# Gated linear attention and a mixture of experts: side jobs of the attention steps stand elsewhere in each engine's order

## Chip, cores and metric

One core of a Trainium2 chip. The metric is the device time of one execution in microseconds (us). Three runs of the kernel before gave 1457.93, 1460.13 and 1462.41 us.

## The reference

```
h = layernorm(x) * (1 + ca) + sa                      # x: 32 x 256 x 128; shifts, scales, gates from c and wmod
q, k, v = h @ W_q, h @ W_k, h @ W_v                   # 16 heads of 64
a = sigmoid(h @ W_gate + b_gate)
S_t = a_t * S_(t-1) + k_t v_t^T ;  o_t = q_t S_t      # a scan over the 256 tokens, per head
x = x + ga * (o @ W_o)
h = layernorm(x) * (1 + cb) + sb
x = x + gb * (shared_expert(h) + sum over the best 2 of 8 experts of weight * expert(h))
```

The recurrence is not run token by token. For chunks of 128 tokens the running products of the gates (F) and their inverses (G) scale queries and keys, and the recurrence becomes masked attention: scores of scaled keys and queries, a causal mask, and a product with the values.

## The kernel before

**Steps and rounds.** The 32 batches have 8 pairs of heads each. One *step* handles two head pairs of one batch, so a batch has 4 steps (`DUOS`, e = 0 to 3), and a *round* of two batches has 8 (s = 0 to 7). 16 rounds make 128 steps, numbered d. Rounds 0, 1, 2 and 15 are written out, 3 to 14 are a loop on each engine. After them a tail finishes the routing and runs the experts block by block.

Every engine has its own order of work, written by hand in its own `round_of_steps`; they meet only through semaphores, and an engine runs in order. A step d is a pipeline over the engines:

- TensorE (PE): attention of step d-1 (`attend`, L1637, into `vo_bank`), scores of step d (L1622), gates of step d+2 (`project_z`, L1534 to L1536 into `z_bank`), queries and keys of step d+1 (`project_qk`, the same lines into `qk_banks`), values (L1577 to L1579, into `vo_bank`) and the output projection of step d-1 (L1648, into `y_bank`). Before the values it waits until ScalarE has copied the attention out of `vo_bank` (`s_o`).
- VectorE (DVE): `first_head` (masked copy of the first head's scores, L1196, L1198), `products` (scaled keys and queries, L1188; they wait for `project_qk`), `scans` (G in L1176, F in L1181, for step d+2).
- ScalarE (ACT): copy of the attention (L767), second head's scores (L785, L786), exponents (L746) and tanh (L752) of the gates, copy of the values (L758), scaled keys for the second chunk (L779).
- GpSimd (POOL): causal mask of the second head (`mask_second_head`, L510; `attend` waits for it), `growth` (L600), `gates` (L593 after the exponents, L595 after tanh; the scans wait for them).
- SyncE (SP) moves rows between memories, one round at a time.

**Side jobs** stand inside these steps. They are the normalisation of the next batch (e = 0 and 1: `normalise`, two transposes L1531, `h_attention` L763, `split_h`) with `moments` and `inverse_std`, and the routing of finished batches: `moments2`, `inverse_std2`, `normalise2` (L1108) and `h_rows` (L567 to L571) make the second layer norm, `h_transposed` (L1531, copied by ACT in L792) transposes it at s = 6 and 7, `router` (L1594, s = 0) and `logits` (L1115) give logits, `logits_exp` (L576) their exponentials, `choose` and `weigh` (s = 3) the two experts of a token and their weights, `ranks` (PE, L1600 to L1607, s = 4) and `places` (DVE, L1156 to L1168, with `next_row` in L1160) the row each token goes to. ACT writes the first expert into the rows (`write_first_expert`, L816, L817), and POOL scatters them with 8 indirect DMAs a round (`scatter_rows`, L584). `update_x` (L614, L617) adds the attention's output to x.

The products of five of these jobs (two normalisations, two transposes of rows, the router, and the ranks) go into `vo_bank`, which the values then take. So PE waits for the engine that reads them (`s_hf`, `s_hc`, `s_lg`, `s_pos`) before the values:

```
                    if s == 4 and two:
                        ranks(i - 1)
                        pe.wait_ge(s_pos, i - 1)
...
                    if ahead:
                        values(1 if e < 2 else 0, e % 2, half if e < 2 else 1 - half)
```

Of the kernel before, what the change touches and what calls it, by code (L numbers as in the profile page):

```python
# [42 lines left out]
def block_kernel(nc, x, W_q, W_k, W_v, W_gate, b_gate, W_o, shared_gate, shared_up, shared_down,  # L43
# [11 lines left out]
    with ctx:  # L55
# [250 lines left out]
        def _(sp):  # L306
# [87 lines left out]
            with growing(sp):  # L394

                sp.dma_start(token_rows[:, :, :], new_rows[:, :, :]).then_inc(s_yc, 16)
                sp.wait_ge(s_xn2, ROUNDS)
# [100 lines left out]
        def _(pool):  # L498
# [61 lines left out]
            def h_rows(b, r, u, k):  # L560
# [5 lines left out]
                alone(s_xn2, k)  # L566
# [52 lines left out]
            def round_of_steps(i, last):  # L619
# [3 lines left out]
                for s in range(2 * DUOS):  # L623
# [13 lines left out]
                    if s == 5 and one:  # L637
                        h_rows((i - 1) * 2 + 1, i - 1, 1, i)
                    if s >= 5 and two:
                        scatter_rows(i - 1, s_fill, (i - 1) * 16, ((0,), (1, 2, 3), (4, 5))[s - 5])  # L640
# [5 lines left out]
                    if s == 4 and one:  # L646
                        h_rows((i - 1) * 2, i - 1, 0, i)
# [84 lines left out]
        def _(sc):  # L732
# [99 lines left out]
            def round_of_steps(i, last):  # L832
                one = not (isinstance(i, int) and i < 1)
                two = not (isinstance(i, int) and i < 2)
                for s in range(2 * DUOS):
# [8 lines left out]
                    second_head(d)  # L844
                    if e == 1 and not (last and half == 1):
                        h_attention(b + 1, b + 2)
                    if s >= 6 and one:
                        copy_h(i, (s - 6) * 2)
                    if ahead:
                        exponents(d + 2, p)  # L850
                        tanh_of(d + 2, p, 0)
                        copy_v(d + 3, 1 if e < 2 else 0, e % 2)
                    if not (last and s == 2 * DUOS - 1):
                        carry_keys(d + 1)
                    if ahead:
                        tanh_of(d + 2, p, 1)
                    if s == 4 and two:
                        write_first_expert(i - 1)
# [128 lines left out]
        def _(dve):  # L987
# [112 lines left out]
            def normalise2(b, u, k):  # L1100
# [9 lines left out]
                if u == 1:  # L1110
                    ins.then_inc(s_xn2, 1)
# [88 lines left out]
            def round_of_steps(i, last):  # L1200
                one = not (isinstance(i, int) and i < 1)
                two = not (isinstance(i, int) and i < 2)
                for s in range(2 * DUOS):
# [3 lines left out]
                    first_head(d)  # L1207
                    if not (last and s == 2 * DUOS - 1):
                        products(d + 1)
                    if s == 0 and two:  # L1210
                        logits(i - 1)
                    if e == 0 and more:
                        normalise(b * CHUNKS + CHUNKS, s_rs, b + 2, s_xn)
                    if e == 1 and more:
                        split_h((1 - half) * T, b + 2)
                    if s == 3 and two:
                        choose(i - 1)
# [3 lines left out]
                    if s == 4 and two:  # L1221
                        places(i - 1)
                    if s == 4 and one:
                        for u in range(2):
                            normalise2((i - 1) * 2 + u, u, i)
                    if s == 7:
                        moments2(b - 1, 0, i + 1)
                    if e == 3 and not last:
# [298 lines left out]
        def _(pe):  # L1527
# [125 lines left out]
            def round_of_steps(i, last):  # L1653
                one = not (isinstance(i, int) and i < 1)
                two = not (isinstance(i, int) and i < 2)
                for s in range(2 * DUOS):
# [12 lines left out]
                    if not (last and s == 2 * DUOS - 1):  # L1669
                        project_qk((e + 1) % DUOS, half if e < 3 else 1 - half)  # L1670
# [4 lines left out]
                    if s == 0 and two:  # L1675
                        router(i - 1)
# [254 lines left out]
```

## Time and profile before

| | us |
|---|---|
| median of 3 runs | 1460.13 |
| the profiled execution | 1457.31 |
| its span, first to last instruction | 1455.2 |
| PE busy | 1251.1 (86%) |
| DVE busy | 1018.9 (70%) |
| POOL busy | 949.2 (65%) |
| ACT busy | 710.3 (49%) |
| mean granted clock of PE | 0.955 of full speed |

The span is that of one profiled execution; the execution's own time is 2.1 us longer. The 128 steps lie between about 20 and 1118 us, the tail after them. The profile names the line and the tiles of each instruction. In a timeline a row is a start, a duration, an engine, a line, and in brackets how long the engine had been idle and which instruction ended that. Several like instructions in a row are merged (x16). PE's durations overlap, since its products are pipelined: distances are taken from start to start. The step that the rows below show is one of round 8, in the loop; "step 2" there means s = 2 of that round.

### The profile page before, as it was taken

What the parts mean: (1) busy time and instruction counts of PE and PEld (TensorE: products, weight loads), DVE (VectorE), ACT (ScalarE), POOL (GpSimd) and SP (SyncE); (2) the same over time, 40 slices, a digit from 0 to 9 for tenths busy, and PEclk for the clock granted to TensorE, in tenths of its full rate; (3) what the DMA queues carried; (4) which work ended last, traced back from release to release, by engine and by line L of the source; (5) the groups of instructions that cost most, each with busy time, mean ns of one, the idle gap of its engine ahead of it and who ended that gap; (6) DMA issues with size and microseconds to landing.
All of it is one profiled execution on the core that took longest, in us unless ns stands there. A gap on an engine that the chain in (4) does not pass through costs nothing. (4 is left out here: it accounts for less than half of the span.)

```text
span 1455.2 us, 35430 instructions
## 1 busy us (share of the span) xinstructions
PE 1251.1 (86%) x10935; PEld 1086.1 (75%) x10935; DVE 1018.9 (70%) x2183; ACT 710.3 (49%) x1637; POOL 949.2 (65%) x1288
## 2 busy tenths in 40 slices
PE   6999888989888888898989798989797989999970
PEld 5888777777777777776878686868686879889860
DVE  6777767666767676677676666667675647788757
ACT  4665554555454555454545454545454444444420
POOL 4356676758585757676767676766667637777755
PEclk9999999999999999999999999999999999999995
DMA  8900102020111202020202020202021136665336
GB/s 241 262 6 25 60 20 80 23 74 32 65 54 42 83 13 96 2 94 2 94 6 91 7 89 7 89 7 89 17 81 66 49 114 197 192 186 177 100 121 227
DMA packets 88445, 119.30 MB, mean 82 GB/s; under 512 B 9652, under 2 KB 52327, under 8 KB 88384
## 3 DMA queue, kind: packets, MB, share of 16 engines
q1 hardware_dynamic: 79296, 101.47, 22.1%
q0 software_dynamic: 9088, 17.07, 3.4%
q8 instruction: 31, 0.51, 0.1%
q14 instruction: 30, 0.25, 0.1%
HBM read 50.29 MB, written 61.79 MB: 77 GB/s over the span
## 5 line engine op out<-in xcount | busy, mean ns | idle before, releaser
L1188 DVE TENSOR_TENSOR pairs<-qk_banks,pairs 128x512 f32<-128x512 f32 x256 | 164.9, 686 | 131.4 <-PE qk_banks L1536 131.3
L595 POOL TENSOR_SCALAR pairs<-pairs 128x512 f32<-128x512 f32 x128 | 91.8, 717 | 197.7 <-ACT pairs L752 197.4
L1637 PE MATMUL vo_bank<-A,shared 128*64 128x256 f32 (+1 forms) x2048 | 202.6, 342 | 15.4 <-POOL A L510 14.6
L1176 DVE TENSOR_TENSOR_SCAN pairs<-pairs,shared 128x515 f32<-128x515 f32 x128 | 161.7, 1264 | 73.3 <-POOL pairs L593 67.7
L1181 DVE TENSOR_TENSOR_SCAN pairs<-pairs,shared 128x515 f32<-128x515 f32 x128 | 170.4, 1331 | 48.6 <-POOL pairs L595 48.6
L710 POOL DMA_INDIRECT y_dram<-pairs,y_row x156 | 158.0, 1013 | 68.4 <-issue 44.2
L1622 PE MATMUL score_banks<-pairs 64*128 64x128 f32 x2048 | 192.6, 286 | 3.2 <-ACT kx L779 3.2
L1637 PEld LDWEIGHTS vo_bank<-A,shared 128*64 128x64 f32 x2048 | 132.3, 141 | 72.7 <-issue 23.7
L1622 PEld LDWEIGHTS score_banks<-pairs 64*128 64x128 f32 x2048 | 146.6, 188 | 25.6 <-issue 25.6
L1577 PE MATMUL vo_bank<-big,h_hi 128*128 128x512 f32 x128 | 63.4, 495 | 117.9 <-DVE next_row L1160 66.5
L758 ACT ACTIVATE shared<-vo_bank 128x512 f32<-128x512 f32 x128 | 76.4, 597 | 168.9 <-PE vo_bank L1579 168.9
L1648 PEld LDWEIGHTS y_bank<-wo,shared 128*128 128x128 f32 x1024 | 146.1, 206 | 15.3 <-ACT h_tile L792 1.9
L584 POOL DMA_INDIRECT rows_dram<-token_rows,dest x120 | 134.0, 1117 | 34.2 <-issue 32.0
L1648 PE MATMUL y_bank<-wo,shared 128*128 128x128 f32 x1024 | 146.9, 291 | 2.1 <-ACT h_tile L792 1.4
L1534 PE MATMUL qk_banks<-h_hi,big 128*128 128x256 f32 x512 | 144.7, 283 | 0.0
L1536 PE MATMUL qk_banks<-h_hi,big 128*128 128x256 f32 x512 | 144.5, 282 | 0.0
L1535 PE MATMUL qk_banks<-h_lo,big 128*128 128x256 f32 x512 | 144.4, 282 | 0.0
L767 ACT ACTIVATE shared<-vo_bank 128x512 f32<-128x512 f32 x128 | 76.4, 597 | 138.7 <-PE vo_bank L1637 138.7
L1577 PEld LDWEIGHTS vo_bank<-big,h_hi 128*128 128x128 f32 x128 | 25.1, 196 | 134.7 <-DVE next_row L1160 67.7
L752 ACT ACTIVATE pairs<-z_bank,half_bg 128x256 f32<-128x256 f32 x256 | 120.2, 470 | 0.0
L510 POOL TENSOR_SCALAR_AFFINE_SELECT A<-A 128x256 f32<-128x256 f32 x256 | 99.3, 413 | 26.0 <-ACT A L786 25.4
L576 POOL TENSOR_TENSOR lg_e<-inv_e,lg 128x8 f32<-128x8 f32 x64 | 105.6, 1664 | 9.3 <-DVE lg L1115 9.3
(252 smaller groups left out, 3241.2 us busy)
## 6 DMA issues: line engine op xcount, KB each, us to landing
rows_dram<-pad_row SPq DMA_DIRECT2D x17, 2112.0 KB, 8.0
ga_all<-rows_dram SPq DMA_DIRECT2D x39, 264.0 KB, 2.8
pairs<-y_dram SPq DMA_DIRECT2D x16, 512.0 KB, 5.0
pairs<-in_L_ffn_gate_w_dram SPq DMA_DIRECT2D x39, 128.0 KB
pairs<-in_L_ffn_up_w_dram SPq DMA_DIRECT2D x39, 128.0 KB
ga_all<-in_L_ffn_down_w_dram SPq DMA_DIRECT2D x39, 128.0 KB, 2.6
mod_rows<-mod_rows_dram SPq DMA_DIRECT2D x32, 128.0 KB, 3.2
h_all<-h_tile SPq DMA_DIRECT2D x16, 256.0 KB, 2.3
```

The source lines that it names most:

```text
L584: g.indirect_dma_start(rows_dram, bass.IndirectOffsetOnAxis(ap=places[:, m:m + 1], axis=0), rows[:, m % PT, :], None, bounds_check=ROWS - ...
L710: g.indirect_dma_start(y_dram, bass.IndirectOffsetOnAxis(ap=y_row[:, u, n:n + 1], axis=0), y_out[:, u, n, :], None, bounds_check=TOKENS * ...
L752: ins = a.activation(th[:, u, :], Z[:, u * T:(u + 1) * T], ACT.Tanh, scale=0.5, bias=half_bg[:, p + u:p + u + 1])
L1176: v.tensor_tensor_scan(G[:, 0:WIDE - 1], gi_t[:, 0:WIDE - 1], cap[:, 0:WIDE - 1], 1.0, ALU.mult, ALU.min)
L1181: v.tensor_tensor_scan(F[:, 0:WIDE - 1], ga_t[:, 0:WIDE - 1], restart[:, 0:WIDE - 1], 1.0, ALU.mult, ALU.add).then_inc(s_fg, 1)
L1188: v.tensor_tensor(out[:, :, :].rearrange("p u (c t) -> p u c t", c=CHUNKS), QKS[:, :, off:off + T].rearrange("p u (c t) -> p u c t", c=CHU ...
L1534: t.matmul(dst, hi, m_hi, start=True, stop=False)
L1535: t.matmul(dst, hi, m_lo, start=False, stop=False)
L1536: return t.matmul(dst, lo, m_hi, start=False, stop=True)
L1622: last = t.matmul(S[:, first:first + P], keys[rows, :], queries[rows, :], start=True, stop=True)
L1637: last = t.matmul(VO[h * DK:(h + 1) * DK, u * T + k * P:(u + 1) * T], v_sb[:, k, vcols], blocks.rearrange("p c t -> p (c t)"), start=(k == ...
L1648: last = t.matmul(Y[:, k * D:(k + 1) * D], oT[:, u * T + k * P:u * T + (k + 1) * P], wo[:, 2 * e + u, :], start=(e == 0 and u == 0 and k = ...
```

## The change

It computes the same. What moves:

- PE: a side job's products now come between the gates and the queries and keys; the wait for the answer stays before the values. The wait for `s_o` moves ahead of the side job with them.
- DVE: `choose`, `normalise2` (from s = 4 to 5), `normalise`, `logits`, `split_h` and `places` come ahead of `products`; `weigh`, `moments2` and `moments` stay behind. `moments` is done at e = 2 instead of 3, but for the first batch.
- ACT: the exponents come ahead of `h_attention` and `copy_h`, both tanh directly behind, ahead of the copy of the values; `write_first_expert` ahead of the exponents.
- POOL: `h_rows` of the first batch at the end of s = 5 instead of 4, of the second at the start of s = 6 instead of 5; the scatters of s = 5, 6, 7 and 0 are 2, 2, 2, 2 instead of 1, 3, 2, 2.
- `normalise2` signals after each of its two batches (`s_xn2`), and `h_rows` waits for its own alone. SP's wait in a branch that is taken only where gates grow beyond a limit counts accordingly.

```diff
@@ POOL, h_rows
-                alone(s_xn2, k)
+                alone(s_xn2, k * 2 - 1 + u)
@@ POOL, round_of_steps
-                    if s == 5 and one:
+                    if s == 6 and one:
                         h_rows((i - 1) * 2 + 1, i - 1, 1, i)
                     if s >= 5 and two:
-                        scatter_rows(i - 1, s_fill, (i - 1) * 16, ((0,), (1, 2, 3), (4, 5))[s - 5])
+                        scatter_rows(i - 1, s_fill, (i - 1) * 16, ((0, 1), (2, 3), (4, 5))[s - 5])
                     mask_second_head(d)
...
-                    if s == 4 and one:
+                    if s == 5 and one:
                         h_rows((i - 1) * 2, i - 1, 0, i)
@@ ACT, round_of_steps
                     second_head(d)
+                    if s == 4 and two:
+                        write_first_expert(i - 1)
+                    if ahead:
+                        exponents(d + 2, p)
                     if e == 1 and not (last and half == 1):
                         h_attention(b + 1, b + 2)
                     if s >= 6 and one:
                         copy_h(i, (s - 6) * 2)
                     if ahead:
-                        exponents(d + 2, p)
                         tanh_of(d + 2, p, 0)
+                        tanh_of(d + 2, p, 1)
+                    if ahead:
                         copy_v(d + 3, 1 if e < 2 else 0, e % 2)
                     if not (last and s == 2 * DUOS - 1):
                         carry_keys(d + 1)
-                    if ahead:
-                        tanh_of(d + 2, p, 1)
-                    if s == 4 and two:
-                        write_first_expert(i - 1)
@@ DVE, normalise2
-                if u == 1:
-                    ins.then_inc(s_xn2, 1)
+                ins.then_inc(s_xn2, 1)
@@ DVE, round_of_steps
                     first_head(d)
+                    if s == 3 and two:
+                        choose(i - 1)
+                    if s == 5 and one:
+                        for u in range(2):
+                            normalise2((i - 1) * 2 + u, u, i)
+                    if e == 0 and more:
+                        normalise(b * CHUNKS + CHUNKS, s_rs, b + 2, s_xn)
+                    if s == 0 and two:
+                        logits(i - 1)
+                    if e == 1 and more:
+                        split_h((1 - half) * T, b + 2)
+                    if s == 4 and two:
+                        places(i - 1)
                     if not (last and s == 2 * DUOS - 1):
                         products(d + 1)
...
-                    if e == 3 and not last:
+                    if e == (3 if isinstance(b, int) and b == 0 else 2) and not last:
@@ PE, round_of_steps
                         project_z((e + 2) % DUOS, half if e < 2 else 1 - half)
-                    if not (last and s == 2 * DUOS - 1):
-                        project_qk((e + 1) % DUOS, half if e < 3 else 1 - half)
                     if begun:
                         pe.wait_ge(s_o, d)
...
                     if s == 0 and two:
                         router(i - 1)
+                    if e == 1 and not (last and half == 1):
+                        xn_transposed(VO, s_xn, b + 2, s_T)
+                    if s == 4 and two:
+                        ranks(i - 1)
+                    if s >= 6 and one:
+                        h_transposed(i, (s - 6) * 2)
+                    if not (last and s == 2 * DUOS - 1):
+                        project_qk((e + 1) % DUOS, half if e < 3 else 1 - half)
+                    if s == 0 and two:
                         pe.wait_ge(s_lg, i - 1)
                     if e == 1 and not (last and half == 1):
-                        xn_transposed(VO, s_xn, b + 2, s_T)
                         pe.wait_ge(s_hf, b + 2)
                     if s == 4 and two:
-                        ranks(i - 1)
                         pe.wait_ge(s_pos, i - 1)
                     if s >= 6 and one:
-                        h_transposed(i, (s - 6) * 2)
                         pe.wait_ge(s_hc, (i - 1) * PT + (s - 6) * 2 + 2)
```

Some lines stand one or two lines further down in the changed file (L1536 there is L1535 here).

How this stands in the programs, at three places of the loop's round. First PE in step 4 of the kernel before, from the last products of queries and keys over the ranks (`picked`, `counting`) to the values:

```order
L1535 MATMUL qk_banks<-h_lo,big 128x256
L1536 MATMUL qk_banks<-h_hi,big 128x256
L1600 MATMUL vo_bank<-picked,counting 128x32
L1604 MATMUL vo_bank<-picked,counting 128x24
L1604 MATMUL vo_bank<-picked,counting 128x16
L1604 MATMUL vo_bank<-picked,counting 128x8
L1607 MATMUL vo_bank<-picked,counting 128x8 x4
L1577 MATMUL vo_bank<-big,h_hi 128x512
```

and the same step of the changed one, from the last products of the gates:

```order
L1536 MATMUL z_bank<-h_lo,big 128x256
L1537 MATMUL z_bank<-h_hi,big 128x256
L1601 MATMUL vo_bank<-picked,counting 128x32
L1605 MATMUL vo_bank<-picked,counting 128x24
L1605 MATMUL vo_bank<-picked,counting 128x16
L1605 MATMUL vo_bank<-picked,counting 128x8
L1608 MATMUL vo_bank<-picked,counting 128x8 x4
L1535 MATMUL qk_banks<-h_hi,big 128x256
```

The twelve products of queries and keys have changed places with the ranks and now lie between the ranks and the values.

Second DVE in step 4, from the first head on; before:

```order
L1198 COPY_PREDICATED A<-causal,score_banks 128x256
L1188 TENSOR_TENSOR pairs<-qk_banks,pairs 128x512 x2
L1019 ISA
L1019 TENSOR_SCALAR xn<-xs,mv,rstd 128x128
...
L1156 TENSOR_TENSOR place_e<-vo_bank,next_row 128x32
L1001 ISA
L1160 TENSOR_TENSOR next_row<-next_row,vo_bank 128x8
```

and changed:

```order
L1198 COPY_PREDICATED A<-causal,score_banks 128x256
L1020 ISA
L1020 TENSOR_SCALAR xn<-xs,mv,rstd 128x128
...
L1156 TENSOR_TENSOR place_e<-vo_bank,next_row 128x32
L1002 ISA
L1160 TENSOR_TENSOR next_row<-next_row,vo_bank 128x8
...
L1168 CAST dest<-place_f 128x8
L1188 TENSOR_TENSOR pairs<-qk_banks,pairs 128x512 x2
```

The scaled keys and queries (L1188) have gone behind the places; in step 3 they have gone behind `choose` in the same way.

Third POOL from the gates of step 5 to the mask of step 6; before:

```order
L593 TENSOR_SCALAR pairs<-pairs 128x4x128
L595 TENSOR_SCALAR pairs<-pairs 128x4x128
L584 DMA rows_dram<-token_rows,dest 73216x132 x3
L542 REGISTER_ALU
L510 AFFINE_SELECT A<-A 128x2x128 x2
```

and changed:

```order
L593 TENSOR_SCALAR pairs<-pairs 128x4x128
L595 TENSOR_SCALAR pairs<-pairs 128x4x128
L542 REGISTER_ALU
L567 ISA
L567 COPY new_rows<-token_ids 128x2
L569 TENSOR_TENSOR new_rows<-new_rows,mod_rows 128x2x128
L571 TENSOR_TENSOR new_rows<-new_rows,mod_rows 128x2x128
...
L584 DMA rows_dram<-token_rows,dest 73216x132 x2
L542 REGISTER_ALU
L510 AFFINE_SELECT A<-A 128x2x128 x2
```

The rows of h of both batches (the second batch's three rows are left out here) now stand between these gates and this mask, with two scatters instead of three; before they stood in steps 4 and 5.

## Rows read from the trace of the kernel before

**Rows 1.** Waits over the whole span: waiting engine, tile, line, releaser: us, times, longest.
```profile
PE vo_bank L1577 <- DVE next_row L1160: 66.5, 14, 5.1
...
PE vo_bank L1577 <- ACT h_full L763: 23.8, 31, 0.8
...
PE vo_bank L1577 <- ACT h_tile L792: 15.8, 28, 0.6
...
PE vo_bank L1637 <- POOL A L510: 14.6, 15, 1.9
...
PE vo_bank L1577 <- DVE lg L1115: 11.0, 14, 0.8
```

**Rows 2.** Timeline of PE, step 2: start us, us, engine, line, operation [idle, releaser].
```profile
580.58 1.52 PE L1637 MATMUL vo_bank<-A,shared 128*64 128x256 f32 x16
...
584.38 0.28 PE L1534 MATMUL qk_banks<-h_hi,big 128*128 128x256 f32 x1
...
585.81 0.40 PE L1577 MATMUL vo_bank<-big,h_hi 128*128 128x512 f32 x1
...
587.49 1.52 PE L1637 MATMUL vo_bank<-A,shared 128*64 128x256 f32 x16
```

**Rows 3.** Timeline of PE, step 4, around the ranks, and step 5's start.
```profile
599.63 0.19 PE L1600 MATMUL vo_bank<-picked,counting 128*128 128x32 bf16 x1
...
604.90 0.80 PE L1577 MATMUL vo_bank<-big,h_hi 128*128 128x512 f32 x1 [4.91 <-DVE next_row L1160]
...
608.18 2.44 PE L1637 MATMUL vo_bank<-A,shared 128*64 128x256 f32 x16
```

**Rows 4.** Timeline of DVE, steps 3 and 4.
```profile
593.01 1.29 DVE L1188 TENSOR_TENSOR pairs<-qk_banks,pairs 128x512 f32<-128x512 f32 x2 [1.25 <-PE qk_banks L1536]
594.22 0.17 DVE L1124 TENSOR_SCALAR lg<-lg_e 128x32 f32<-128x32 f32 x1
...
596.25 0.17 DVE L1139 CAST top_f<-top_i 128x8 f32<-128x8 uint32 x1
...
598.09 0.48 DVE L1008 BATCH_NORM_STATS2 stats<-xs 128x6 f32 x2
...
599.20 1.23 DVE L1176 TENSOR_TENSOR_SCAN pairs<-pairs,shared 128x515 f32<-128x515 f32 x1 [0.28 <-issue]
...
601.47 0.70 DVE L1196 COPY_PREDICATED A<-causal,score_banks 128x512 f32<-128x512 int32 x1
...
603.59 0.89 DVE L1019 TENSOR_SCALAR xn<-xs,mv,rstd 128x128 f32 x2
...
604.68 0.16 DVE L1160 TENSOR_TENSOR next_row<-next_row,vo_bank 128x8 f32<-128x8 f32 x1
```

**Rows 5.** Windows: stretch, busy us per engine, granted clock (PEclk, 1.00 is 2.4 GHz), DMA.
```profile
604.90:608.20 3.30, 3.30 (x13) 2.80 (x13) 0.36 (x3) 1.62 (x6) 0.00 (x0) 0.50 0.00 0
193.00:196.72 3.72, 1.86 (x12) 1.57 (x12) 1.51 (x4) 2.60 (x8) 3.13 (x7) 1.00 0.05 18
```

**Rows 6.** Timeline of PE, round 15, after the ranks.
```profile
1094.12 0.50 PE L1577 MATMUL vo_bank<-big,h_hi 128*128 128x512 f32 x1 [2.92 <-DVE next_row L1160]
```

**Rows 7.** Timeline of ACT, step 5.
```profile
615.34 0.83 ACT L746 ACTIVATE pairs<-z_bank,neg_bg 128x256 f32<-128x256 f32 x2
```

**Rows 8.** Timeline of POOL, steps 5 to 7.
```profile
610.26 0.85 POOL L567 COPY new_rows<-token_ids 128x2 f32 x1 [1.37 <-DVE new_rows L1108]
...
615.64 1.10 POOL L584 DMA_INDIRECT rows_dram<-token_rows,dest  x1 [0.29 <-issue]
...
623.31 0.77 POOL L510 TENSOR_SCALAR_AFFINE_SELECT A<-A 128x256 f32<-128x256 f32 x2
...
626.66 0.62 POOL L595 TENSOR_SCALAR pairs<-pairs 128x512 f32<-128x512 f32 x1 [1.25 <-ACT pairs L752]
...
632.04 0.80 POOL L510 TENSOR_SCALAR_AFFINE_SELECT A<-A 128x256 f32<-128x256 f32 x2
```

**Rows 9.** One line: the second scan, duration ns min/median/max, first and last start.
```profile
L1181 DVE TENSOR_TENSOR_SCAN pairs<-pairs,shared x128: 1197/1230/1697, 20.9 to 1108.5; 128x515 f32<-128x515 f32 x128
```

More of the change, by code:

```diff
@@ L396, in _ @@
                 sp.dma_start(token_rows[:, :, :], new_rows[:, :, :]).then_inc(s_yc, 16)
-                sp.wait_ge(s_xn2, ROUNDS)
+                sp.wait_ge(s_xn2, ROUNDS * 2)
                 sp.wait_ge(s_xu, B + 1)
@@ L1207, in round_of_steps @@
                     first_head(d)
+                    if s == 3 and two:
[11 more added lines that the diff above has]
+                        places(i - 1)
                     if not (last and s == 2 * DUOS - 1):
                         products(d + 1)
[L1210 to L1215, printed above, removed]
                     if s == 3 and two:
-                        choose(i - 1)
                         weigh(i - 2, i - 1)
@@ L1220, in round_of_steps @@
                         moments2(b - 1, 1, i)
[L1221 to L1225, printed above, removed]
                     if s == 7:
                         moments2(b - 1, 0, i + 1)
-                    if e == 3 and not last:
+                    if e == (3 if isinstance(b, int) and b == 0 else 2) and not last:
                         if isinstance(b, int) and b == 0:
```

## The prediction

> **What bounds the kernel now.** I read the page first, for where the time lies: 128 steps between 20 and about 1118 us, then a tail of about 340 us that the change does not touch. Inside the steps the timeline of PE tells most. A step without a side job takes 587.49 - 580.58 = 6.91 us [rows 2], and PE has no gap in it: 3.80 us of attention, scores and gates, 1.43 of queries and keys, 1.68 of values and output. So PE sets the pace there, and what counts elsewhere is only what makes PE wait. The waits view names it [rows 1]: PE stood before the values (L1577) for 66.5 us in 14 rounds until DVE had updated `next_row`, 23.8 until ACT had made `h_full`, 15.8 until ACT had copied `h_tile`, 11.0 until DVE had read the logits; before the attention (L1637) it stood 14.6 us for POOL's mask. Together 131.7 us.
>
> All but the last have one shape: a side job's products go into `vo_bank`, another engine answers, and PE waits at once, since the values need that bank and the queries and keys are already done. Step 4 shows it at its worst [rows 3]: the ranks go out at 599.63, the values start at 604.90, 4.91 us of that idle. The reason stands on DVE [rows 4]: in step 3 it does the expert choice, the weights and both moments behind the products, starts its scans at 599.20, and reaches step 4's first head at 601.47 and `next_row` at 604.68.
>
> The stall costs twice. After it the granted clock is 0.50 [rows 5], the lower level of 1.2 GHz. Values and output take 608.18 - 604.90 = 3.28 us instead of 1.68, and the attention after them 2.44 instead of 1.52 [rows 2, 3]: 2.52 us more a round.
>
> **Part by part.**
>
> *PE: side job ahead of queries and keys.* No product is added. Between a side job and its answer 1.43 us of PE work now lie, where PE had none. The waits for `h_full`, `h_tile` and the logits averaged 0.77, 0.56 and 0.79 us [rows 1]. ACT now does two exponents first (0.83 us [rows 7]), but they can start when the gates are done, beside the side job itself; at worst 0.79 + 0.83 - 1.43 = 0.2 us is left, at best nothing. I take nothing: 50.6 us gone.
>
> *DVE: choice ahead of the products, moments one step earlier.* Ahead of the products DVE sat idle 1.25 us for PE [rows 4]. The choice (596.25 - 594.22 = 2.03) fills that and delays step 3's products by 0.78. Behind them the weights and `moments2` (598.09 - 596.25 = 1.84) and the scans (601.47 - 599.20 = 2.27) remain; `moments` (599.20 - 598.09 = 1.11) is gone to step 2. Step 3's attention starts at 587.49, its products end 6.73 us later; now 7.51, and the scans at 7.51 + 1.84 + 2.27 = 11.62. From the first head to `next_row` DVE took 604.68 - 601.47 = 3.21, of which 1.21 was products that now come after: 2.00. So `next_row` starts 13.62 us after step 3's start, 6.71 after step 4's, and PE goes on 0.22 later (604.90 against 604.68): 6.93. PE itself is there at 3.80 + 0.3 for the ranks (an estimate from rows 3: 604.90 less the 4.91 idle, less 599.63) + 1.43 = 5.5. About **1.4 us remain** of 4.9, 14 times 1.4 = 20 us.
>
> *The clock.* After 1.80 us for a mask the granted clock was still 1.00 [rows 1, 5]; after 2.92 us in round 15 the records slowed again a little later [rows 6]. 1.4 lies below the first, so I take the clock as kept: 14 times 2.52 = 35.3 us gained. The other end is nothing.
>
> *ACT.* The second tanh comes ahead of the copy of the values, so the second gate is ready earlier; in rows 8 POOL waited 1.25 for it in step 7. Nobody on PE's path waited for that, so nothing is counted, but it gives POOL room. The wait for the copied output (`s_o`) moves ahead of the queries and keys; that copy follows the attention, at the step's start, with over 2 us of scores and gates to cover it.
>
> *POOL: scatters 2, 2, 2, 2 instead of 1, 3, 2, 2; rows of h in steps 5 and 6.* POOL runs in order, and the mask (L510) that the attention needs stands behind these jobs. Both halves of `h_rows` took 615.64 - 0.29 - 610.26 = 5.09 us, a scatter 1.10 + 0.29 = 1.39, the mask 0.77 [rows 8]. In step 5 POOL's gates now end about 6.9 us in, an estimate: 3.80 to PE's gates, five ACT instructions (exponents, `h_full`, tanh) at 0.42 [rows 7], POOL's 0.62 [rows 8], some 0.4 for the hand-overs. Then 5.09 of rows, two scatters at 1.39 and the mask: 15.5 us after step 5's start, 8.4 after step 6's if step 5 takes 7.16 (6.91 and some 0.25 for two transposes, estimated from the 12 products of queries and keys in 1.43). The next attention is due at 7.16: PE waits about 1.2. From step 6's mask to step 7's POOL took 632.04 - 623.31 = 8.73, of which 1.25 was that tanh: 7.48 against a step of 7.16, 0.3 more. Then scans and POOL collide: the second scan takes 1197 ns at best and 1697 at worst [rows 9]; late gates bring that about, and I take one such half microsecond a round. Sum 2.0, bounds 1.2 and the 4.4 of the rival below; 14 times 2.0 = 28 us. The old mask wait of 14.6 is gone with the old order.
>
> *Other waits.* `normalise2` signals each half, and the first rows of h wait for the first only: no cost, DVE's gap ahead of the products covers the four instructions. SP's extra count of `s_xn2` is in a branch that does not run. The first experts' copy (two short ACT instructions) moves ahead of the exponents in step 4, where ACT idled; it frees DVE's wait for it before `dest`, which now would stand ahead of the products.
>
> **Sum.** 131.7 + 35.3 = 167 us can go at most; 20 (ranks) and 28 (masks) come back: 119 us. The profiled run took 1457.31 us: 1338. The median of the runs is 2.8 us higher, which makes 1341; the removed terms are from one run, so I say **1340 us**. About 0.3% is what a measurement here can tell from no change.
>
> **The rivals.**
>
> 1. *PE is all but unbroken.* Rows of h run at their undisturbed speed while DVE is in the first head, and the mask is in time; only the ranks' 1.4 is left. 167 - 20 = 147: 1313 us with the median's offset. For it: POOL idled 1.25 for tanh alone in a step [rows 8]. Against: the mask already came late in 15 rounds [rows 1]. Chance 0.14.
>
> 2. *DVE and POOL shut each other out.* Denser steps put gates and scans on top of each other: in steps 6 and 7 one POOL job waits for a whole scan (1.2 us [rows 9]). That is 2.4 more a round, 4.4 in all, 34 us: 1374. The scan's 0.5 us spread over the minimum shows that something of the kind exists. The Trainium skill, "SBUF — State Buffer", section "Who interferes with whom", says that a DVE instruction with two SBUF inputs and a GpSimd instruction that reads SBUF exclude each other, and that the later one blocks fully; by it the packing of this change would be worse than my sum. Rows 9 agree with it in kind; how often it happens in the new order, no row here tells. Chance 0.14.
>
> 3. *The clock still falls* after the remaining stalls (1.4, and up to 2 for a mask, near the 2.92 of rows 6): 35 us come back, 1375. Against: 1.80 us left it at 1.00. Chance 0.07.
>
> 4. *The change does not do what it says at the ranks:* `next_row` stays as late, because DVE's chain is longer than I think. The 66.5 us and the clock's 35 stay, the masks' 28 come: 167 - 66.5 - 35 - 28 = 38 gained, 1422. Against: 3 us of work visibly leave the stretch. Chance 0.03.
>
> 5. *Slower: POOL becomes the bound in steps 6, 7 and 0.* Each holds two scatters ahead of the mask. In the sum they cost 1.39 us each; every microsecond more is paid six times a round, or 84 us in 14 rounds. From 2.8 us each (1.4 more, 119 us) the gain is gone; at 3.3 the time is 1500. For it: scatters are issued closer together. Against: the one in rows 8 took 1.10 with 0.29 of issue among other work. Chance 0.02.
>
> **How the numbers follow.** The main case has 0.60, between about 1322 (masks at 1.2, no collision) and 1360 (1.4 more a round, at ranks or masks, is 20). The range 1312 to 1375 takes in rivals 1 to 3 at their centres, leaves out their outer halves, 4 and 5. Faster by over 0.3%: all but rival 5 and a sliver: 0.97; within 0.3%: 0.01; slower: 0.02.
>
> **What would show it.** Right: the wait for `next_row` falls to about 1.4 us each, those for `h_full`, `h_tile` and logits vanish, steps 2 and 3 stay at 6.91 us, the clock after the ranks is 1.00, and PE's main wait is for L510 in step 7. Wrong: a granted clock of 0.50 after step 4; a step without side job longer than 6.91; or POOL's mask waits above 4 us a round.

## The result, and the profile after

The changed kernel took 1335.45 us (median of 4 runs, 1333.73 to 1339.03) beside 1459.45 for the kernel before (4 runs, 1457.93 to 1462.41). The ratio is 0.9151, 95% interval 0.9127 to 0.9175: 124 us less. Forecast were 1340, range 1312 to 1375. The profiled execution took 1335.02 us, its span 1332.9, the mean granted clock 0.979 against 0.955.

First the waits view over the whole span of the changed kernel (waiting engine, tile, line, releaser: us, times, longest). The changed code stands a line or so further down: L1577 is now L1578, L1637 is L1638, L1019 is L1020.

```profile
PE vo_bank L1638 <- POOL A L510: 26.7, 27, 2.4
...
PE vo_bank L1578 <- DVE next_row L1160: 25.0, 14, 2.2
...
POOL pairs L595 <- ACT pairs L752: 9.4, 19, 0.6
```

Against [rows 1], the waits for `h_full`, `h_tile` and the logits are gone, the one for `next_row` fell from 66.5 us to 25.0, the one for the mask rose from 14.6 to 26.7. The last row, POOL's second gate waiting for ACT's second tanh, fell most; before, it was:

```profile
POOL pairs L595 <- ACT pairs L752: 197.4, 111, 3.9
```

Next the timeline of PE, steps 4 to 7 of round 8 (start, us, engine, line, idle before and its end).

```profile
535.19 1.52 PE L1638 MATMUL vo_bank<-A,shared 128*64 128x256 f32 x16
539.00 0.19 PE L1601 MATMUL vo_bank<-picked,counting 128*128 128x32 bf16 x1
542.81 0.50 PE L1578 MATMUL vo_bank<-big,h_hi 128*128 128x512 f32 x1 [1.94 <-DVE next_row L1160]
544.59 1.52 PE L1638 MATMUL vo_bank<-A,shared 128*64 128x256 f32 x16
548.40 0.38 PE L1532 MATMUL vo_bank<-ident,xn 128*128 128x128 f32 x2
550.05 0.40 PE L1578 MATMUL vo_bank<-big,h_hi 128*128 128x512 f32 x1
551.73 1.52 PE L1638 MATMUL vo_bank<-A,shared 128*64 128x256 f32 x16
...
560.17 1.52 PE L1638 MATMUL vo_bank<-A,shared 128*64 128x256 f32 x16 [1.25 <-POOL A L510]
```

Distances between attentions are the steps: step 4 has 9.40 us, step 5 7.14, step 6 8.44. Values, output and attention behind the ranks are at full speed again (1.78 and 1.52 us, against 3.28 and 2.44 in [rows 3]). Steps 2 and 3 stayed at 6.91. All eight steps of such a round take 61.6 us; before they took 70.1, so the 12 rounds of the loop give 102 of the 124 us.

On the timeline of DVE one sees why step 4 still waits:

```profile
534.56 1.28 DVE L1188 TENSOR_TENSOR pairs<-qk_banks,pairs 128x512 f32<-128x512 f32 x2
...
536.81 0.49 DVE L1093 BATCH_NORM_STATS2 stats<-xs 128x6 f32 x2
...
537.94 1.23 DVE L1176 TENSOR_TENSOR_SCAN pairs<-pairs,shared 128x515 f32<-128x515 f32 x1 [0.29 <-issue]
...
540.21 0.72 DVE L1196 COPY_PREDICATED A<-causal,score_banks 128x512 f32<-128x512 int32 x1
...
541.14 1.25 DVE L1020 TENSOR_SCALAR xn<-xs,mv,rstd 128x128 f32 x2
...
542.59 0.16 DVE L1160 TENSOR_TENSOR next_row<-next_row,vo_bank 128x8 f32<-128x8 f32 x1
...
553.34 1.69 DVE L1181 TENSOR_TENSOR_SCAN pairs<-pairs,shared 128x515 f32<-128x515 f32 x1
```

From the products to `next_row` the only idle time that the view marks on DVE is 0.29 us ahead of the first scan. And the timeline of POOL shows what the mask of step 6 stands behind (ranks' step 4, then step 5 and 6):

```profile
541.11 0.62 POOL L593 TENSOR_SCALAR pairs<-pairs 128x512 f32<-128x512 f32 x1
541.70 0.62 POOL L595 TENSOR_SCALAR pairs<-pairs 128x512 f32<-128x512 f32 x1
...
550.78 0.72 POOL L595 TENSOR_SCALAR pairs<-pairs 128x512 f32<-128x512 f32 x1 [0.49 <-ACT pairs L752]
551.45 0.18 POOL L567 COPY new_rows<-token_ids 128x2 f32 x1
...
552.48 1.47 POOL L571 TENSOR_TENSOR new_rows<-new_rows,mod_rows 128x256 f32<-128x256 f32 x1
553.89 1.12 POOL L567 COPY new_rows<-token_ids 128x2 f32 x1
...
555.86 0.74 POOL L571 TENSOR_TENSOR new_rows<-new_rows,mod_rows 128x256 f32<-128x256 f32 x1
556.85 1.04 POOL L584 DMA_INDIRECT rows_dram<-token_rows,dest  x1 [0.25 <-issue]
558.19 0.97 POOL L584 DMA_INDIRECT rows_dram<-token_rows,dest  x1 [0.30 <-issue]
559.16 0.77 POOL L510 TENSOR_SCALAR_AFFINE_SELECT A<-A 128x256 f32<-128x256 f32 x2
```

Gates, rows of h, two scatters, mask: nothing between them but 0.25 to 0.49 us of issue and of waiting for tanh, and PE waits 1.25 us for the last. Within the rows of h one product takes 1.47 us and one copy 1.12, where others of their kind take 0.74 and 0.18: the two slow ones run beside the scans of DVE (552.14 to 555.03 us).

### The profile page after: what moved, and what is told of

Read it like the earlier page. It is cut to its first block and busy times, and to the rows that moved or that the text cites. A ratio compares the mean times of both kernels' runs of the same rounds, so it can differ in the third digit from the quotient of the medians.

```text
span 1332.9 us, 35442 instructions
## 1 busy us (share of the span) xinstructions
PE 1209.7 (91%) x10935; PEld 1063.2 (80%) x10935; DVE 1039.1 (78%) x2183; ACT 717.1 (54%) x1637; POOL 946.5 (71%) x1288
## 5 line engine op out<-in xcount | busy, mean ns | idle before, releaser
L1188 DVE TENSOR_TENSOR pairs<-qk_banks,pairs 128x512 f32<-128x512 f32 x256 | 164.5, 684 | 82.0 <-PE qk_banks L1537 81.5
L1638 PE MATMUL vo_bank<-A,shared 128*64 128x256 f32 (+1 forms) x2048 | 197.0, 335 | 27.5 <-POOL A L510 26.7
L1176 DVE TENSOR_TENSOR_SCAN pairs<-pairs,shared 128x515 f32<-128x515 f32 x128 | 174.2, 1361 | 36.3 <-POOL pairs L593 30.1
L1638 PEld LDWEIGHTS vo_bank<-A,shared 128*64 128x64 f32 x2048 | 129.3, 138 | 81.7 <-issue 24.0
L1181 DVE TENSOR_TENSOR_SCAN pairs<-pairs,shared 128x515 f32<-128x515 f32 x128 | 167.8, 1311 | 0.0
L584 POOL DMA_INDIRECT rows_dram<-token_rows,dest x120 | 124.9, 1041 | 58.3 <-issue 31.5
L1535 PE MATMUL qk_banks<-h_hi,big 128*128 128x256 f32 x512 | 151.8, 297 | 0.0
L1537 PE MATMUL qk_banks<-h_hi,big 128*128 128x256 f32 x512 | 144.3, 282 | 0.0
L1649 PEld LDWEIGHTS y_bank<-wo,shared 128*128 128x128 f32 x1024 | 133.8, 191 | 13.1 <-ACT h_tile L792 1.1
L1536 PE MATMUL qk_banks<-h_lo,big 128*128 128x256 f32 x512 | 144.1, 281 | 0.0
L1649 PE MATMUL y_bank<-wo,shared 128*128 128x128 f32 x1024 | 135.1, 275 | 1.6 <-ACT h_tile L792 0.9
L576 POOL TENSOR_TENSOR lg_e<-inv_e,lg 128x8 f32<-128x8 f32 x64 | 119.2, 1876 | 9.3 <-DVE lg L1115 9.3
L1196 DVE COPY_PREDICATED A<-causal,score_banks 128x512 f32<-128x512 int32 x128 | 93.7, 732 | 29.1 <-PE score_banks L1623 26.7
L746 ACT ACTIVATE pairs<-z_bank,neg_bg 128x256 f32<-128x256 f32 x256 | 107.6, 473 | 6.6 <-PE z_bank L1537 2.9
L785 ACT ACTIVATE A<-score_banks 128x256 f32<-128x256 f32 x128 | 49.2, 385 | 114.4 <-PE score_banks L1623 114.4
L752 ACT ACTIVATE pairs<-z_bank,half_bg 128x256 f32<-128x256 f32 x256 | 108.4, 486 | 0.0
```

The source lines that it names most:

```text
L576: g.tensor_tensor(lg_e[:, n, :], inv_e[:, n, :], lg[:, n, :], ALU.pow).then_inc(s_le, 1)
L584: g.indirect_dma_start(rows_dram, bass.IndirectOffsetOnAxis(ap=places[:, m:m + 1], axis=0), rows[:, m % PT, :], None, bounds_check=ROWS - ...
L1176: v.tensor_tensor_scan(G[:, 0:WIDE - 1], gi_t[:, 0:WIDE - 1], cap[:, 0:WIDE - 1], 1.0, ALU.mult, ALU.min)
L1181: v.tensor_tensor_scan(F[:, 0:WIDE - 1], ga_t[:, 0:WIDE - 1], restart[:, 0:WIDE - 1], 1.0, ALU.mult, ALU.add).then_inc(s_fg, 1)
L1188: v.tensor_tensor(out[:, :, :].rearrange("p u (c t) -> p u c t", c=CHUNKS), QKS[:, :, off:off + T].rearrange("p u (c t) -> p u c t", c=CHU ...
L1535: t.matmul(dst, hi, m_hi, start=True, stop=False)
```

## The experiments

The theory is that of the prediction: PE waits for answers of engines that work in order, the edits move the answers or put PE's work in front of them, and a long wait also costs clock. The rivals are that one edit alone does it, or that the remaining waits have another cause. "Loop round" is one of rounds 3 to 14. The ratios are to the kernel before, timed again with each group of runs: its median was 1461.19 us beside e1 to e4, 1458.56 beside e5 to e8, 1459.18 beside e9 and e10, and 1458.51 beside e11 and e12.

### e1: the changed kernel with PE's order of before

```diff
+                    if not (last and s == 2 * DUOS - 1):
+                        project_qk((e + 1) % DUOS, half if e < 3 else 1 - half)
                     if begun:
                         pe.wait_ge(s_o, d)
...
                         router(i - 1)
...
                         ranks(i - 1)
                         pe.wait_ge(s_pos, i - 1)
...
-                    if not (last and s == 2 * DUOS - 1):
-                        project_qk((e + 1) % DUOS, half if e < 3 else 1 - half)
```

> The changed kernel with TensorE's order of before: side jobs stand behind the queries and keys again, the other engines keep the new order. Theory 1 (PE sets the pace and each answer is hidden by the 1.43 us of queries and keys): the old waits come back, 50.6 us for h_full, h_tile and logits, while the ranks' wait stays near 1.9 us, since DVE's chain sets next_row; about 1386 us, and waits for h_full 0.77, h_tile 0.56, logits 0.79 us each. Theory 2 (the shorter chains on DVE, ACT and POOL carry the gain, PE's order is worth little): 1335 to 1345 us.

1383.66 us, ratio 0.9472 [0.9449, 0.9495], close to the theory's 1386. The waits of PE:

```profile
PE vo_bank L1578 <- DVE next_row L1160: 26.6, 14, 2.3
PE vo_bank L1578 <- ACT h_full L763: 23.8, 31, 0.8
PE vo_bank L1578 <- ACT h_tile L792: 15.8, 28, 0.6
...
PE vo_bank L1578 <- DVE lg L1115: 5.0, 14, 0.4
```

`h_full` and `h_tile` are back to the tenth of a microsecond of [rows 1]. The wait for `next_row` hardly moved (25.0 to 26.6): there DVE's chain ends late, whatever PE does in between, so it was not PE's order that shortened it from 66.5. Three things were not expected. The wait for the logits came back only half (11.0 before), since DVE still answers ahead of its products. The wait for the mask fell from 26.7 to 4.9 us: steps 6 and 7 take 8.33 and 7.93 us, in the changed kernel 8.44 and 7.83, so there the wait for `h_tile` and the one for the mask only change places, and PE's order brings nothing. And the clock fell behind the ranks in five loop rounds. The time thus came near the forecast by terms that partly cancel.

### e2 and e10: the kernel before with PE's order of the change

```diff
e2: PE's order of the change, nothing else
e10: e2, and on DVE
                     first_head(d)
+                    if s == 0 and two:
+                        logits(i - 1)
                     if not (last and s == 2 * DUOS - 1):
                         products(d + 1)
-                    if s == 0 and two:
-                        logits(i - 1)
```

> The kernel before with TensorE's new order alone. Theory 1: the three waits of 50.6 us go; next_row comes as late as before, so its 4.9 us a round and the clock's fall stay; about 1409 us, 1405 to 1425. Theory 2: within a few us of 1459. A third view, that PE's order alone brings all of it, says 1335 to 1350.

1436.78 us, ratio 0.9842 [0.9825, 0.9858]: a miss, PE's order alone brings 24 us, half of what undoing it costs. Its waits:

```profile
PE vo_bank L1577 <- DVE next_row L1160: 64.9, 14, 5.0
PE vo_bank L1637 <- POOL A L510: 35.1, 27, 3.4
PE vo_bank L1577 <- DVE lg L1115: 22.1, 14, 1.6
```

and DVE in step 0:

```profile
625.66 1.29 DVE L1188 TENSOR_TENSOR pairs<-qk_banks,pairs 128x512 f32<-128x512 f32 x2 [1.86 <-PE qk_banks L1536]
626.87 0.18 DVE L1115 TENSOR_TENSOR lg<-vo_bank,rbias 128x32 f32<-128x32 f32 x1
```

The logits, ready at PE, stand on DVE behind products that now wait for queries and keys that PE does after the router. So their wait doubled, 11.0 to 22.1. Nor did step 5 gain (9.67 us on average, before 9.71): the wait for `h_full` is gone there, but the mask's ahead of the next attention has grown. e10 tries the reason given for the logits:

> The kernel before with TensorE's new order (e2), and the logits put ahead of the products on VectorE at step 0. If the 22.1 us that TensorE waits for the logits in e2 come from logits standing behind products that themselves wait for the queries and keys, they go: 1436.8 - 22 = about 1415, with the waits for next_row (64.9) and the masks (35.1) as in e2. Rival: the products get late instead and TensorE waits for exponents or weights, about 1437.

1415.48 us, ratio 0.9696 [0.9681, 0.9711], as expected to the microsecond: no row of the logits is left among PE's waits, and `next_row` stands at 64.9 as in e2. The exactness is luck: the mask's wait is 30.4 us and not 35.1, and the clock fell in step 6 in five loop rounds (8.7 us instead of 7.15), in e2 in none. The two edits belong together: for the logits, PE's order pays only where DVE answers ahead of its products.

### e3: choice of experts behind the products

```diff
-                    if s == 3 and two:
-                        choose(i - 1)
                     if not (last and s == 2 * DUOS - 1):
                         products(d + 1)
...
                     if s == 3 and two:
+                        choose(i - 1)
                         weigh(i - 2, i - 1)
```

> The changed kernel with the choice of step 3 behind the products again. next_row comes 2.03 - 0.78 = 1.25 us later, so the wait at the ranks grows from 1.8 to about 3.1 us a round. Theory 1 with the clock falling after a wait of that length (2.92 did it in the kernel before, 1.94 did not in the changed one): 14 times 1.25 and 14 times 2.5 us more, about 1387 us, with 0.50 granted after step 4. Without a fall of the clock: 1353 us.

1368.35 us, ratio 0.9364 [0.9348, 0.938], between the two. The wait for `next_row` is 42.9 us (14 times, 3.4 at most), 1.3 more each as the theory has it. The clock fell in 10 of the 12 loop rounds; a round with a fall took 64.5 us, one without 62.9, so a fall costs 1.6 here and not 2.5. This PE timeline has one round of each, values and attention after it:

```profile
623.43 0.50 PE L1577 MATMUL vo_bank<-big,h_hi 128*128 128x512 f32 x1 [3.22 <-DVE next_row L1160]
625.46 2.83 PE L1637 MATMUL vo_bank<-A,shared 128*64 128x256 f32 x16
...
687.88 0.50 PE L1577 MATMUL vo_bank<-big,h_hi 128*128 128x512 f32 x1 [3.22 <-DVE next_row L1160]
689.66 1.52 PE L1637 MATMUL vo_bank<-A,shared 128*64 128x256 f32 x16
```

The same wait of 3.22 us, once with the attention slowed to 2.83 us and once not.

### e4: scatters 1, 3, 2, 2 as before

```diff
-   scatter_rows(i - 1, s_fill, (i - 1) * 16, ((0, 1), (2, 3), (4, 5))[s - 5])
+   scatter_rows(i - 1, s_fill, (i - 1) * 16, ((0,), (1, 2, 3), (4, 5))[s - 5])
```

> The changed kernel with the scatters of steps 5, 6, 7, 0 as 1, 3, 2, 2. Theory 1 (POOL's work between the gates of step 5 and the mask of step 6 is what PE waits for in step 7): one scatter of 1.3 us more there, the wait for the mask grows from 1.25 to about 2.5 us: 1335 + 14 times 1.3 = 1353 us, or 1388 if the clock falls after 2.5 us. Theory 2 (POOL has room, the mask wait comes from elsewhere): 1335 us.

1370.21 us, ratio 0.9384 [0.9369, 0.94], again between the bounds with and without the clock. Step 6 takes 9.74 instead of 8.44: 1.30, one scatter. The rest is clock: it fell in step 7 of 10 of the 12 loop rounds, where a step then takes 8.73 instead of 7.84, and in step 4 of six.

### e8: ACT's order as before, but for the first experts' copy

```diff
                         write_first_expert(i - 1)
-                    if ahead:
-                        exponents(d + 2, p)
                     if e == 1 and not (last and half == 1):
                         h_attention(b + 1, b + 2)
                     if s >= 6 and one:
                         copy_h(i, (s - 6) * 2)
                     if ahead:
+                        exponents(d + 2, p)
                         tanh_of(d + 2, p, 0)
-                        tanh_of(d + 2, p, 1)
-                    if ahead:
                         copy_v(d + 3, 1 if e < 2 else 0, e % 2)
                     if not (last and s == 2 * DUOS - 1):
                         carry_keys(d + 1)
+                    if ahead:
+                        tanh_of(d + 2, p, 1)
```

> The changed kernel with ScalarE's order of before (exponents behind h_attention and the copy of h, the second tanh behind the copy of the values and the scaled keys); the first experts' copy stays where the change put it. The prediction counted this order at nothing. Theory 1 as predicted: 1335 to 1340 us. Theory 1 with POOL as the second limit: POOL's second gate waits 1.2 to 1.5 us longer for tanh in each step, and in steps 5 to 7 that time goes straight on to the masks: 14 times 1.5 = 21 us, about 1356 us, and up to 1378 with a fall of the clock in each round.

1385.0 us, ratio 0.9498 [0.948, 0.9517]: ACT's order, which the prediction counted at nothing, is worth 50 us in the changed kernel, and the time is above the 1378 us expected at most. POOL's timeline from step 5's second gate, in a round whose step 5 starts at 565.55, says how:

```profile
574.25 0.90 POOL L595 TENSOR_SCALAR pairs<-pairs 128x512 f32<-128x512 f32 x1 [2.12 <-ACT pairs L752]
575.11 0.18 POOL L567 COPY new_rows<-token_ids 128x2 f32 x1
```

The rows of h begin 9.56 us into the step, in the changed kernel 551.45 - 544.59 = 6.86. All that follows on POOL is late by that: PE waited 33.8 us for masks, 14.6 for POOL's rows ahead of their transposes, and 30.0 for `next_row`, and in most rounds steps 4 and 6 took 10.1 and 10.9 us.

### e5, e6 and e7: the two waits that are left

```diff
e5, on DVE:
+                    if s == 4 and two:
+                        places(i - 1)
                     if e == 0 and more:
                         normalise(b * CHUNKS + CHUNKS, s_rs, b + 2, s_xn)
...
-                    if s == 4 and two:
-                        places(i - 1)
e6, on POOL: scatters 2, 1, 2, 2, 1 over s = 5, 6, 7, 0, 1 in place of 2, 2, 2, 2
e7: e5 and e6
```

> The changed kernel with the places of step 4 ahead of the normalisation (which PE needs only in step 5). In the changed kernel's trace the normalisation stood 1.17 us ahead of them (541.14 to 542.31 us). Theory 1 (DVE's chain to next_row sets the ranks' wait): the wait falls from 1.8 to about 0.7 us, 14 times 1.17 = 16 us, about 1319 us. Theory 2 (the wait is set elsewhere, by the ranks themselves or by the choice): 1335 us.

e5: 1321.68 us, ratio 0.9061 [0.9046, 0.9076]. The wait for `next_row` fell to 10.4 us, step 4 to 8.25, while the masks' stayed (26.5). So the normalisation's 1.25 us did stand in PE's way.

> The changed kernel with the 8 scatters of a round as 2, 1, 2, 2, 1 over steps 5, 6, 7, 0, 1 instead of 2, 2, 2, 2. Theory 1 (POOL's queue ahead of the mask is what PE waits for in steps 6 and 7): one scatter of 1.28 us less ahead of step 6's mask takes the wait of 1.25 us there, and 0.66 behind step 7 falls with the backlog; the mask waits fall from 27 to under 8 us, 1313 to 1320 us. Theory 2 (scans and POOL shut each other out there, so the order of the scatters matters little): 1330 to 1336 us.

e6: 1330.67 us, ratio 0.9125 [0.9111, 0.9138], as the rival says, though the mask wait fell as planned, from 26.7 to 8.7 us. The gain was given back in step 4: the wait for `next_row` rose a little, to 28.8, and after it the clock fell in 7 of the 12 loop rounds (step 4 then took 10.9 to 11.3 us instead of 9.72), in the changed kernel in one. The sum agrees: 18.0 us of mask waits gone, 3.8 more for `next_row`, six more falls at 1.5, so 5 are left of 18, and 4.8 were measured.

> Both of these moves together. Theory 1: PE is left with the rest of the ranks' wait alone, the gains add: 16 + 18 = 34 us, about 1301 us (1296 to 1306). If they share a cause, they do not add: 1315 us.

e7: 1306.57 us (1304.62 to 1307.05), ratio 0.8952 [0.8939, 0.8965], just above the range expected: 28.9 us less than the changed kernel, not 34, but more than e5 and e6 by themselves (13.8 and 4.8). The clock fell in no loop round, and a round takes 59.4 us. With the ranks' wait shortened first, the scatters bring 15.1 us: the mask's wait falls by 17.8 (26.5 to 8.7), the one for `next_row` rises by 3.6 (10.4 to 14.0).

### e9, e11 and e12: what is left of step 4

```diff
e9: e7, and on DVE (inverse_std2 on POOL from s = 4 to 5, behind the scatters)
-                    if s == 3 and one:
-                        moments2(b - 1, 1, i)
+                    if s == 4 and one:
+                        moments2(b - 2, 1, i)
e11: e9, and on DVE
-                    if s == 5 and one:
-                        for u in range(2):
-                            normalise2((i - 1) * 2 + u, u, i)
...
                         products(d + 1)
+                    if s == 5 and one:
+                        for u in range(2):
+                            normalise2((i - 1) * 2 + u, u, i)
e12: e11, scatters 2, 0, 2, 2, 2 over s = 5, 6, 7, 0, 1
```

> On top of e7 the statistics of the second row statistic (moments2, some 0.8 to 0.9 us of VectorE) leave step 3 and stand in step 4 behind the products, and inverse_std2 goes from step 4 to step 5 behind the scatters. If VectorE's chain into next_row is still what sets step 4, some 0.8 us a loop round go, 14 rounds, 1306.6 - 11 = about 1296. Rival: what needs inverse_std2 (the row of POOL's step 5) gets it too late, POOL's step shifts, and the time stays at 1306 or rises, with TensorE's wait for POOL's mask above the 8.7 us of e7.

e9: 1298.68 us (1296.27 to 1301.18), ratio 0.8903 [0.889, 0.8916], the fastest of all. The time came out, the path did not. Step 4 lost 1.35 us (8.55 to 7.2, no wait left), step 7 lost 0.65, but step 6 gained 1.37, in a wait that was not there:

```profile
PE score_banks L1625 <- ACT kx L781: 21.6, 14, 3.2
```

The moments moved into a stretch in which DVE has no gap either, and with `normalise2` ahead of step 5's products the scaled keys come late. So the step I expected gave more, and another took as much back.

> On top of e9, the normalisation of the rows of h (normalise2, 2.00 us of VectorE at step 5) stands behind step 5's products. In e9 TensorE waits 1.5 us a round in step 6 for the scaled keys (kx), because the products come after it on VectorE; that wait should go. GpSimd then gets the rows some 0.7 us later, so its mask of step 6 is ready about 0.75 us after the next attention is due: step 6 falls from 8.55 to about 7.9, 14 rounds, 1298.7 - 9 = about 1290, with a mask wait of about 0.75 a round in place of the wait for kx. Rival: the mask (it ended 1.37 us before the attention that the late kx delayed) is itself what binds once GpSimd's jobs shift by the full 1.3 us of products, and the time stays at 1299.

e11: 1320.28 us, ratio 0.9045 [0.903, 0.906], a miss in the wrong direction: the wait for `kx` did go (3.2 left, all outside the loop), but step 6 rose to 9.12. On POOL, the copy and the first product of the rows of h, in e11:

```profile
603.62 1.37 POOL L567 COPY new_rows<-token_ids 128x2 f32 x1 [0.91 <-DVE new_rows L1111]
604.95 1.70 POOL L569 TENSOR_TENSOR new_rows<-new_rows,mod_rows 128x256 f32<-128x256 f32 x1
```

and in e9:

```profile
592.79 0.18 POOL L567 COPY new_rows<-token_ids 128x2 f32 x1
592.95 0.76 POOL L569 TENSOR_TENSOR new_rows<-new_rows,mod_rows 128x256 f32<-128x256 f32 x1
```

In e11 they start later and fall beside the two scans of DVE (603.78 to 606.13 us), where these two take 2.1 us longer. PE now waits for the rows themselves (14.2 us before the transposes of step 6) and for masks (16.6).

> On top of e11, the scatter of step 6 goes to step 1 (2, 0, 2, 2, 2 over steps 5, 6, 7, 0, 1). It is 1.82 us on GpSimd plus 0.17 before it in e9, ahead of step 6's mask; a second scatter at step 1 costs GpSimd some 1.3 us where it has slack. If the mask binds step 6 in e11, the wait for it goes: another 0.5 to 0.75 us a round, about 1280 to 1284. Rival: step 1 becomes tight on GpSimd (its mask late), or the binding thing in step 6 is VectorE's first head, and the time is that of e11.

e12: 1313.42 us, ratio 0.8995 [0.898, 0.9011], 7 us less than e11 but far above the 1280 to 1284 expected, which had counted on e11's own forecast. The waits:

```profile
PE vo_bank L1534 <- POOL new_rows L571: 14.3, 13, 1.1
PE vo_bank L1640 <- POOL A L510: 12.0, 13, 0.9
```

Step 7 came to 7.13 and step 6 to 8.46, but step 1 to 8.14 instead of 7.14, by the mask that now stands behind two scatters there: the rival holds for step 1. The rows before the transposes wait for no scatter, so nothing changed there. e9 remains the best.

## Why the prediction was right

The likeliest case came true, 1335 against 1340: the waits behind side jobs went, the clock was mostly kept, and two smaller waits came in their place. That the number came within 5 us is in part luck: terms missed by more than that in both directions and cancelled (the last item). By its steps:

- **Side-job waits, 50.6 us gone.** Shown: three rows of the waits view are gone, and e1 brings two of them back unchanged and the logits by half. The 15.8 us of `h_tile` were no gain by themselves, though: e1 shows that PE would wait for the mask in their place. In step 1 the gain was even a little more than the idle time. In [rows 1] a wait for `h_full` is 0.77 us (23.8 over 31), but the step went from 8.21 to 7.14, by 1.07.
- **Ranks, 1.4 us forecast, 1.79 measured** (25.0 over 14; 1.94 in the round shown). `next_row` starts 542.59 - 535.19 = 7.40 us into step 4 instead of 6.71. Of the 0.69 more, the products' end was right within 0.05 (7.51 forecast; 535.84 - 528.28 = 7.56, the latter being step 3's start). Weights and moments with the 0.29 of issue ahead of the scan make 0.26 more than forecast, and first head to `next_row` 2.38 instead of 2.00: the normalisation, 0.89 in [rows 4], is 1.25 here, with POOL's gates of 541.11 and 541.70 beside it. In e5, where it stands elsewhere, each of its two instructions takes 0.33 to 0.35 us. e5 also shows its place on the path.
- **The clock, 35.3 us forecast, mostly kept.** In the changed kernel it fell after the ranks in one loop round of 12 (round 5). The ground was that a wait below 1.80 us leaves it alone. The second window of [rows 5] ends with that wait; the attention behind it (196.72 to 198.30 us) had 1.00 as well, so the reading holds, but for one wait. As a rule it was too simple: in e4, with the same mean wait of 1.8 us, the clock fell in six rounds. Nothing in the prediction tells these two cases apart, so that it fell in only one here is in part luck (see the last section).
- **Masks, 2.0 us a round forecast, 1.26 + 0.70 measured** (step 6 is 8.44 against 7.18 in e7, step 7 7.83 against 7.13 in e9, where neither waits for a mask). POOL's gates were put at 6.9 us into step 5, and the rows of h began at 6.86; the mask at 15.5 and ended at 559.93 - 544.59 = 15.34. The collision was there, but inside this sum: the second scan at 553.34 takes 1.69 us, and the slow product and copy above cost POOL 1.47 - 0.74 + 1.12 - 0.18 = 1.67 us, more than PE waits for that mask; no run takes this loss away by itself. The forecast had such a loss in its 5.09 us without saying so, since the rows of h in [rows 8] were slowed as well (a copy of 0.85 us there).
- **"Nothing is counted" for ACT: the step of the reasoning that failed**, though not in the sum. The 6.9 us of the POOL term already had both tanh early in it; with ACT's order of before that is 9.56, and e8 is 50 us slower. "Nobody on PE's path waited for that" was read from the profile of before, in which POOL's jobs stood elsewhere; after the change POOL is on PE's path in steps 5 to 7.
- **Rival 2**, DVE and POOL shutting each other out in a whole scan, did not come about in the changed kernel at the price given: the mask waits are 1.9 a round and not 4.4. Its mechanism is there, as the 1.67 us above show, and more of it costs time: e11 packs the two so, and a loop round takes 60.3 us instead of 58.8 (not all of it by this, since the rows also start later). The Trainium skill, "SBUF — State Buffer", section "Who interferes with whom", says that DVE and GpSimd share one pair of ports under an exclusive lock. The pairs of rows of e9 and e11 (0.18 to 1.37, 0.76 to 1.70 us) agree in kind.
- **The balance.** 167 us could go. 51.7 remain in the two waits; some 3 went with the clock in rounds 5 and 15. That leaves 112, and the profiled executions differ by 122.3. The other 10 us are not traced. Removed waits brought more than their idle time, about 0.3 each in step 1, which over the 31 waits for `h_full` would be 9 us (an estimate from that step alone).

The parts do not add up: undoing PE's order costs 48 us, ACT's 50, the choice 33, the scatters 35, together 166 of a gain of 124, whereas PE's order alone on the kernel before brings 24. Undoing one of them lengthens waits that the others had shortened, and often brings the clock's fall with it. `moments` one step earlier and the rows of h in steps 5 and 6 are undone in no run, so what these two moves bring by themselves is not shown.

## What to carry to other kernels

Where an in-order engine waits for an answer, put its independent work between question and answer, and on the answering engine put the answer ahead of work that waits for that same independent work: for the logits the second without the first halved the wait (11.0 to 5.0 us, e1), the first without the second doubled it (22.1, e2), and both removed it (e10). Ask too what the engine would wait for next: where that comes as late, as the masks in steps 6 and 7, the move brings nothing. An engine off the path in the profile of before can be on it in the new order, so cost an edit there with the new positions. After each removed wait look at the clock of the stretch behind the next longest one: in e6 it took back half of what the masks had given.

## What the runs showed that was not expected

The clock does not fall by the length of the wait alone. In the changed kernel two rounds have the same wait for `next_row`, 1.94 us at 542.81 and 1.93 here, on the PE timeline of round 5:

```profile
356.47 0.50 PE L1578 MATMUL vo_bank<-big,h_hi 128*128 128x512 f32 x1 [1.93 <-DVE next_row L1160]
358.46 2.83 PE L1638 MATMUL vo_bank<-A,shared 128*64 128x256 f32 x16
```

The windows over the two attentions (busy us of PE, PEld, DVE, ACT and POOL, then the granted clock, where 0.50 is 1.2 GHz and 1.00 is 2.4):

```profile
358.46:361.29 2.83, 2.83 (x19) 1.75 (x18) 2.32 (x3) 0.19 (x1) 1.72 (x2) 0.50 0.14 48
...
544.59:546.11 1.52, 1.52 (x19) 1.06 (x18) 1.52 (x3) 0.40 (x2) 1.22 (x2) 1.00 0.00 0
```

Between kernels a longer wait made falls more frequent, but not by itself. By mean wait for `next_row`, the clock fell behind it in none of the 12 loop rounds at 1.0 us (e7), in one at 1.8 (the changed kernel) but six at 1.8 in e4, five at 1.9 (e1), seven at 2.1 in e6 but four at 2.1 in e8, and 10 at 3.1 (e3). Such a fall cost 1.5 to 1.6 us of a round (e6: 62.08 against 60.59; e3: 64.5 against 62.9). What decides in a single round no run here shows.
